# Which queue issues the transfers of the negated row maxima: SyncE's or ScalarE's

## What is computed

```
# sa: causal, 1024 keys    ca: 154 keys    la: 154 keys, causal
s = einsum('blhd,bmhd->bhlm', q, k)
s = where(mask, s, -inf)
p = softmax(s)                      # exp(s - max over m) / sum
a = einsum('bhlm,bmhd->blhd', p, v)
x = x + a @ wo + bo ;  x = x + gelu(ln(x) @ w1 + b1) @ w2 + b2
```

## Time and profile before

| | us |
|---|---|
| runs | 1113.71, 1117.44, 1120.88 |
| median | 1117.44 |
| span of the profiled execution | 1118.3 |
| TensorE busy | 936.4 |
| VectorE busy | 582.5 |
| ScalarE busy | 419.9 |

### The profile page before, as it was taken

The page is one execution under the profiler, slowest core; times in us unless marked ns, Lnnn a source line. Parts: engine busy times, 40 slices in busy tenths (PEclk is TensorE's granted clock), DMA queues, the critical chain, the costliest instruction groups (busy, mean ns, idle before and its releaser), DMA issues.

```text
span 1118.3 us, 13782 instructions
## 1 busy us (share of the span) xinstructions
PE 936.4 (84%) x5180; PEld 456.9 (41%) x5180; DVE 582.5 (52%) x1347; ACT 419.9 (38%) x822; POOL 73.3 (7%) x83
## 2 busy tenths in 40 slices
PE   3888864899988898888989867999887888987898
PEld 1433322345443353434445324633233454442365
DVE  5555637784667704488545675665125504415500
ACT  1133331342355625353422431167763323343421
POOL 2102000000000200000000001000000000000210
PEclk9988886799999999988999897999998999998999
DMA  7805462202132100645020401013004004022000
GB/s 275 102 1 73 75 139 43 24 2 27 23 38 30 29 1 20 94 51 66 1 30 1 57 13 17 10 40 48 1 20 57 2 1 57 2 37 22 1 19 19
DMA packets 47013, 43.85 MB, mean 39 GB/s; under 512 B 13510, under 2 KB 44386, under 8 KB 46434
## 3 DMA queue, kind: packets, MB, share of 16 engines
q1 hardware_dynamic: 46948, 42.98, 24.0%
HBM read 13.32 MB, written 2.10 MB: 14 GB/s over the span
## 4 chain that ended last, share of the span: by engine, by line
PE 57%; DVE 17%; DMA 10%; ACT 8%; SPq 5%; issue 4%; ACTq 0%; DVEq 0%
PE ps_exp L852 10%; PE ps_o L964 10%; PE ps_misc L835 10%; PE ps_max L889 8%; ACT probs L1200 5%; DVE mcol L1114 5%; SPq L695 4%; PE ps_exp L922 4%; DMA QA<-part 4%; PE ps_chain L814 3%; PE ps_chain L822 3%; DVE swap L1028 2%; DMA QC<-part 2%; PE ps_exp L927 2%; PE ps_chain L787 2%
## 5 line engine op out<-in xcount | busy, mean ns | idle before, releaser
L1114 DVE TENSOR_REDUCE mcol<-ps_max 128x3 f32<-128x462 f32 (+5 forms) x496 | 292.2, 626 | 181.9 <-PE ps_max L891 106.1
L1200 ACT ACTIVATE probs<-ps_exp 128x512 f32<-128x512 f32 (+3 forms) x544 | 261.1, 523 | 242.0 <-PE ps_exp L925 87.0
L889 PE MATMUL ps_max<-KA,QA 96*128 96x512 bf16 (+3 forms) x384 | 117.9, 359 | 55.3 <-DVE mcol L1114 24.4
L922 PE MATMUL ps_exp<-QA,KA 98*128 98x512 bf16 (+3 forms) x384 | 120.4, 350 | 26.1 <-ACT probs L1200 18.3
L835 PE MATMUL ps_misc<-hT,w_up 128*128 128x512 f32 x256 | 125.7, 615 | 7.2 <-ACT hid L1191 2.2
L852 PE MATMUL ps_exp<-w_down,hid 128*128 128x256 f32 x512 | 128.2, 388 | 0.0
L1191 ACT ACTIVATE hid<-ps_misc,col 128x512 f32<-128x512 f32 x64 | 44.0, 687 | 200.4 <-PE ps_misc L835 200.4
L852 PEld LDWEIGHTS ps_exp<-w_down,hid 128*128 128x128 f32 x512 | 94.5, 190 | 29.7 <-issue 15.5
L1248 POOL TENSOR_TENSOR part<-rot,part 128x512 bf16<-128x512 f32 (+1 forms) x36 | 40.8, 1133 | 923.2 <-DVE part L1038 923.2
L889 PEld LDWEIGHTS ps_max<-KA,QA 96*128 96x128 bf16 x384 | 39.2, 104 | 123.1 <-DVE mcol L1114 63.6
L964 PE MATMUL ps_o<-probs,V 128*17 128x512 f32 (+3 forms) x768 | 85.1, 517 | 3.2 <-ACT probs L1200 2.3
(11 more groups left out here) (109 smaller groups left out, 986.6 us busy)
## 6 DMA issues: line engine op xcount, KB each, us to landing
QA<-part SPq DMA_DIRECT2D x72, 128.0 KB, 5.1
QC<-part SPq DMA_DIRECT2D x72, 128.0 KB, 5.2
KA<-part SPq DMA_DIRECT2D x48, 128.0 KB, 5.2
xb<-in_x SPq DMA_DIRECT2D x8, 512.0 KB, 6.1
out<-xb SPq DMA_DIRECT2D x4, 512.0 KB, 3.0
KC<-part SPq DMA_DIRECT2D x24, 77.0 KB, 3.1
w_up<-in_fc SPq DMA_DIRECT2D x1, 1024.0 KB, 7.0
w_down<-in_fc SPq DMA_DIRECT2D x1, 1024.0 KB, 8.2
```

The source lines that it names most:

```text
L889: mm = pe.matmul(dst, q, kk, start=True, stop=not causal)
L922: mm = pe.matmul(bank[:, q0:CH], KA[:, g // NT, hh, (g % NT) * P:(g % NT + 1) * P], QA[:, hh, q0:CH], start=True, stop=(r < 0))
L1114: dve.tensor_reduce(dst, src, AX.X, ALU.max).then_inc(s_max_done, 1)
L1200: act.activation(probs[:, n % 2, h, q0:CH], ps_exp[exp_nth[s] % 2][:, q0:CH], ACT.Exp).then_inc(s_exp_done, 1)
```

## The change

The branch of the step `row` moves from SyncE's program to ScalarE's. The semaphore waited for, the two transfers and what waits for them stay the same. ScalarE's program handles the step at its place in `ORDER`, between its own activations.

```diff
--- before.py
+++ after.py
@@ block.sync
-                elif k == "row":
-                    _, att, c, hg = s
-                    n = item_slot[s[1:]]
-                    after_misc(sp, s)
-                    q, h0 = q_of(att, c), hg * HG
-                    for i in range(2):
-                        sp.dma_start(q[SROW + i:SROW + i + 1, h0:h0 + HG, :],
-                                     mrow[:, n, i, :]).then_inc(s_mput[n], 16)
@@ block.scalar, between the branches of "exp" and "evac"
+                elif k == "row":
+                    _, att, c, hg = s
+                    n = item_slot[s[1:]]
+                    after_misc(act, s)
+                    q, h0 = q_of(att, c), hg * HG
+                    for i in range(2):
+                        act.dma_start(q[SROW + i:SROW + i + 1, h0:h0 + HG, :],
+                                      mrow[:, n, i, :]).then_inc(s_mput[n], 16)
```

## The result

The changed kernel is slower: 1173.74 us median (1167.77 to 1178.12, 4 runs) against 1119.16 (4 runs), ratio 1.049 (95% interval 1.0443 to 1.0537), 54.6 us more. Its profiled execution took 1175.08 us with a span of 1173.3, so what lies around the span is 1.8 us.

The account below looks back on a forecast made before the run. It took no engine as a wall by itself, TensorE coming first at 84% busy. Its terms, 12.1 + 11.7 - 1.0 = 22.8 us on top of 1117.4, gave 1140 us, range 1118 to 1164.

Parts of the forecast that it names:

- late step's credit: The one row step where context key transfers kept SyncE's queue 2.6 us too long: gain of 1.0 us, ends 0 and 2.6.
- Fourteen free steps: Row steps, for instance in the MLP, where ScalarE waits for TensorE anyway: no cost.
- The five steps: Row steps with VectorE far behind in rotary positions or a layer norm while ScalarE runs ahead: 12.1 us together.
- (1): `rot` moved at 119.8 instead of 112.08, so the value projection waits for its bank: 2.0 us.
- (3): `rot` at 557.91 would end at 563.0, where VectorE wanted it at 561.22: 1.8 us.
- How much reaches the end: Delays carried to the end time: 12.1 us taken whole, plus 11.7, half of 23.4, the rest filling gaps.
- the 29 steps: Row steps among exponentials: TensorE 0 to 2.2 us late at each, 0.8 on average, 23.4 us in all.
- TensorE's clock stays as it is: Sign expected in the profile after: TensorE's clock unchanged; longer gaps lowering it were named as a way to be wrong.
- Cheap issue: Rival: ScalarE hands over both transfers in almost no time, only the wait for VectorE is left: 1124 us, chance 0.14.
- The gaps take it: Rival: TensorE's idle time swallows the 23.4 us; only two `rot` delays, 1.8 us each, count: 1118 us, chance 0.12.
- The dearer case: Rival: all 23.4 us count, and issues cost more on ScalarE or VectorE's maxima come later: above 1160, chance 0.12.
- all passed on: Whole 23.4 us reaches the end at 1.16 us of issue per step: 1117.4 + 12.1 + 23.4 - 1.0 = 1152 us.

Follow-up runs that it names:

- e5: Kernel before, plus two extra SBUF-to-SBUF transfers issued on ScalarE at each row step without a wait; real ones stay on SyncE: 1122.12 us, ratio 1.0023.
- e3: Kernel before, with only the five row steps where VectorE is far behind waited for and issued on ScalarE: 1136.79 us, ratio 1.0150.
- e4: Kernel before, with the other 43 row steps on ScalarE and the five where VectorE is far behind left on SyncE: 1149.48 us, ratio 1.0267.
- e2: Kernel before, plus two extra transfers to HBM issued on ScalarE at each row step without a wait: 1119.40 us, ratio 0.9987.
- e12: Kernel before, with the wait and both real transfers moved to GpSimd's program in place of ScalarE's: 1123.73 us, ratio 1.0024.
- e6: Kernel before, plus two extra SBUF-to-SBUF issues on ScalarE at each row step, then the wait for VectorE: 1140.97 us, ratio 1.0186.
- e7: Kernel before, plus the wait for VectorE on ScalarE at each row step, then two extra SBUF-to-SBUF issues: 1181.80 us, ratio 1.0547.

## Why the prediction was wrong

The direction held, and so did the main of the mechanism, a wait and two issues ahead of wanted work on ScalarE; the size was 22.8 us against 54.6, and TensorE's clock was missing. By its steps:

- **SyncE gives back nothing.** Right. The late step's credit of 1.0 is too small to be told in any run.
- **The issue.** 2 x 0.578 = 1.16 us was forecast, and ScalarE takes 1.15 for a pair. The bound of 0 for issues beside a running activation turned out real, but only without a wait ahead of them (e5). Behind the wait the whole 1.16 stands, as the sum had it.
- **Fourteen free steps.** Right. Behind the five in the MLP the distance between the profiles moves by -0.2 to 0.1 us, and behind all fourteen together by -1.6.
- **The five steps.** 12.1 us forecast, 17 measured alone (e3), 18.8 by the shifts. By the shifts (1) was sized too large, 2.0 against 0.7, and the other four too small: 1.8 against 2.8, 1.8 against 4.3, 3.0 against 5.9 and 3.5 against 5.1. At the two before an MLP I let part of the late exponential overlap VectorE's norm. But L964, `evac`, `turn` and `hT` stand in a row behind it, and little of that overlapped. Why (3) cost more than twice what was forecast stays open.
- **How much reaches the end.** This is the step that failed. I took half of the 23.4 us of the 29 steps, 11.7, since gaps would swallow the rest. The 43 steps that hold these 29 cost 30 (e4), and by the shifts the 29 carry 39.6 in the changed kernel, the clock's part included: not only the half was wrong, even the whole 23.4 was too small. No gap swallowed them. By the kernel's waits a delay can come round again: VectorE's maxima need TensorE's matmuls, the row step needs the maxima, and ScalarE now needs the row step. No run takes this ring apart from the clock. Taken whole, 12.1 + 23.4 = 35.5, the reading comes close to the 34.7 us of new idle time on TensorE, but that is largely luck, since both terms were sized too small.
- **"TensorE's clock stays as it is."** Wrong, and the second missing term: 20.3 us more of busy time at a lower granted clock, 0.908 against 0.930. How much of that the end time holds is open (8 us by the estimate above). It was named as what could make the prediction wrong and was given no price and hardly a chance.
- **The rivals.** Cheap issue had 1124 for the wait alone; the wait alone is at 1130, nearly all of it at the five steps, but it isn't what happened, since the issues behind the wait were not cheap. "The gaps take it" fell. The dearer case (above 1160), at a chance of 0.12, is what came. Its "all passed on" gives 1152, 22 us short; the clock and the steps sized too small lie in that, and no run shares it out between them.
- **The rule of the Trainium skill** (DMA: Bandwidth & Descriptors, section Issuing engines are not separate DMA queues): that it saves only the sequencer's time agrees with e2, e5 and e12, all within 0.3% of the kernel before. It says nothing of what a wait ahead of the issue costs the new engine, and wait and issue together were the whole effect (e6, e7).

## What to carry to other kernels

Ask of a moved transfer first what its new engine must wait for before it may issue, and what is queued behind: an issue of 0.58 us was free beside running work, and the same issue behind a wait held back ScalarE's next activation at 32 of 48 steps. If it has to sit on a busy engine, put it some steps later in that engine's list, where its wait is already over; that took 47 of 55 us back. Where engines form a ring (maximum, row, exponential, product), pass a delay on whole, and give a price to a fall of TensorE's granted clock where a stretch gets new idle time.

## What the runs showed of the hardware

- ScalarE's sequencer issues a transfer while an activation is still running (211.13 against an end at 211.36 in e5, and so at 90 of 96 issues there); 96 issues of 0.60 us cost no measurable time.
- Two queues that issue at the same moment can lengthen each other's issues: a pair on ScalarE took 1.41 us in the median beside a pair on SyncE (e7), and 1.15 alone.
- In one stretch of four row steps TensorE's idle time went from 3.7 to 6.0 us, with one gap of 1.70 us ahead of a fall to 1.2 GHz that lasted 10.2 us; the mean granted clock was 0.86 in place of 0.99, and TensorE was busy for 30.9 us in place of 27.9.
- A transfer of 4 KB issued from GpSimd took 0.487 us to issue, as its profile has it, and 1.6 us to land (e12), no slower than from SyncE (0.578 and 1.7) or ScalarE (0.590 and 1.7).
